# A linear-attention block with a sparse feed-forward: casts of weight sums moved ahead, row turns in pairs, and a later end for seven down products

## What is computed

```python
def attn(x, Wq, Wk, Wv, Wo):                 # 16 heads, 4 key/value heads, head size 128
    q, k, v = x @ Wq.T, x @ Wk.T, x @ Wv.T   # split into heads; RoPE on q and k
    qf, kf = elu(q) + 1, elu(k) + 1
    state, z = cumsum_s(kf[s] outer v[s]), cumsum_s(kf[s])
    out[s] = (qf[s] @ state[s]) / (qf[s] . z[s] + 1e-6)
    return out @ Wo.T

def ffn(x, w_gate, w_up, w_down):            # 512 -> 2048 -> 512
    h = silu(x @ w_gate) * (x @ w_up)
    h = keep_the_2_largest_of_every_4(h)     # by absolute value, along the 2048
    return h @ w_down

x = x + layernorm(attn(layernorm(x)))
x = x + layernorm(ffn(layernorm(x)))
```

## Time and profile before

| | |
|---|---|
| median of 3 runs | 1211.42 us (1211.18 to 1211.43) |
| the profiled execution | 1212.48 us |
| its span in the profile | 1210.5 us |
| mean granted TensorE clock | 0.989 of full speed |
| TensorE busy | 1172.4 us, 97% of the span |
| VectorE, ScalarE, GpSimd busy | 863.9, 521.0, 472.9 us (71%, 43%, 39%) |

### The profile page before, as it was taken

The page is one execution under the profiler, slowest core; times in us unless marked ns, Lnnn a source line. Parts: engine busy times, 40 slices in busy tenths (PEclk is TensorE's granted clock), DMA queues, the critical chain, the costliest instruction groups (busy, mean ns, idle before and its releaser), DMA issues.

```text
span 1210.5 us, 16282 instructions
## 1 busy us (share of the span) xinstructions
PE 1172.4 (97%) x5862; PEld 985.0 (81%) x5862; DVE 863.9 (71%) x1428; ACT 521.0 (43%) x1017; POOL 472.9 (39%) x381
## 2 busy tenths in 40 slices
PE   9999999999999999999999989798999999999986
PEld 7888888888888888888888778686888787888865
DVE  8944666756665457676576777888687778868798
ACT  5534544544545345444455333434423444333322
POOL 6421533525645125153355334453434533212224
PEclk9999999999999999999999989999999999999998
DMA  6321423313344133232246867665523564343421
GB/s 222 87 68 51 105 66 79 100 37 102 120 121 124 48 88 88 69 88 75 54 138 189 281 209 237 219 214 182 157 87 113 197 207 162 122 156 122 156 70 70
DMA packets 96367, 153.77 MB, mean 127 GB/s; under 512 B 10272, under 2 KB 31008, under 8 KB 96288
## 3 DMA queue, kind: packets, MB, share of 16 engines
q1 hardware_dynamic: 96288, 152.74, 40.9%
HBM read 96.60 MB, written 40.89 MB: 114 GB/s over the span
## 4 chain that ended last, share of the span: by engine, by line
PE 74%; DVE 15%; ACT 4%; issue 3%; DMA 1%; SPq 1%; POOL 1%; DVEq 0%; ACTq 0%
PE bank_q L812 8%; PE bank_q L814 8%; PE bank_q L813 8%; PE bank_y L814 5%; PE bank_y L813 5%; PE bank_y L812 5%; PE bank_od L1040 5%; PE bank_od L1043 4%; PE bank_t L812 3%; PE bank_t L814 3%; PE bank_t L813 3%; PE bank_s L937 2%; PE bank_s L812 2%; PE bank_s L813 2%; PE bank_s L814 2%
## 5 line engine op out<-in xcount | busy, mean ns | idle before, releaser
L812 PE MATMUL bank_q<-x_hi,w_hi 128*128 128x512 f32 x464 | 187.0, 403 | 1.0 <-ACT scratch L1343 0.9
L814 PE MATMUL bank_q<-x_lo,w_hi 128*128 128x512 f32 x464 | 182.0, 392 | 0.0
L813 PE MATMUL bank_q<-x_hi,w_lo 128*128 128x512 f32 x464 | 181.7, 392 | 0.0
L1944 POOL TENSOR_TENSOR w_lo<-stage,w_hi 128x512 fp32r<-128x512 f32 x60 | 78.8, 1323 | 123.8 <-ACT w_hi L1216 123.1
L1944 POOL TENSOR_TENSOR big_lo<-q_rows,big_hi 128x1024 fp32r<-128x1024 f32 x31 | 73.9, 2385 | 116.8 <-ACT big_hi L1255 116.8
L1944 POOL TENSOR_TENSOR big_lo<-hidden,big_hi 128x512 fp32r<-128x512 f32 x24 | 46.4, 1954 | 147.8 <-ACT big_hi L1389 100.2
L814 PEld LDWEIGHTS bank_q<-x_lo,w_hi 128*128 128x128 f32 x464 | 87.7, 189 | 19.1
L812 PEld LDWEIGHTS bank_q<-x_hi,w_hi 128*128 128x128 f32 x464 | 87.8, 189 | 18.3 <-ACT scratch L1343 1.8
L813 PEld LDWEIGHTS bank_q<-x_hi,w_lo 128*128 128x128 f32 x464 | 87.9, 189 | 16.8
L814 PE MATMUL bank_y<-wout_lo,a_hi 128*128 128x512 f32 x256 | 100.0, 391 | 0.0
L812 PE MATMUL bank_y<-wout_hi,a_hi 128*128 128x512 f32 x256 | 99.8, 390 | 0.0
(11 more groups left out here) (423 smaller groups left out, 3063.7 us busy)
## 6 DMA issues: line engine op xcount, KB each, us to landing
q_rows<-scratch SPq DMA_DIRECT2D x116, 128.0 KB, 2.4
x_rows<-x SPq DMA_DIRECT2D x40, 256.0 KB, 2.9
stage<-wq SPq DMA_DIRECT2D x32, 256.0 KB, 2.8
stage<-wo SPq DMA_DIRECT2D x32, 256.0 KB, 2.7
s_keep<-x_hi SPq DMA_DIRECT2D x16, 512.0 KB, 4.3
s_keep<-x_lo SPq DMA_DIRECT2D x16, 512.0 KB, 5.2
w_hi<-s_keep SPq DMA_DIRECT2D x32, 256.0 KB, 3.6
w_lo<-s_keep SPq DMA_DIRECT2D x32, 256.0 KB, 4.1
```

The lines of the kernel that those rows point to most:

```text
L812: pe.matmul(ps, whi, xhi, start=first, stop=False, skip_group_check=True)
L813: pe.matmul(ps, wlo, xhi, start=False, stop=False, skip_group_check=True)
L814: return pe.matmul(ps, whi, xlo, start=False, stop=last, skip_group_check=True)
L1944: return pool.tensor_tensor(dst, full, hi.bitcast(F32), ALU.subtract)
```

## The change

It has three parts.

1. ScalarE's cast of the sums of round r moves from the end of its slot S[r] + 1 to near its head, behind the casts of weights for down products and ahead of the absolute value. In `SUM_AT`, rounds 10 to 15 go from slots 13, 14, 15, 17, 18, 19 to 12, 13, 14, 15, 17, 18; by the formula above their loads, casts, low parts and stores move with them.
2. The eight row turns of the second batch go from slots 19, 20, 20, 21, 22, 23, 23, 24 into pairs in slots 19, 21, 23, 25; statistics and normalising move accordingly, and so do five of the first six steps of `combine_x` (from slots 25 to 27 into 26 and 27).
3. Down product 49 goes from slot 62 to slot 64, where six others already stand. VectorE adds it up at the head of slot 64 instead of in slot 63; in slot 64 three sums instead of one stand between the masks and the kept rows; the last kept rows and their low parts move from slot 66 to slot 65 on VectorE, as do the matching casts on ScalarE and the piece of this work on GpSimd.

```diff
--- before.py
+++ after.py
@@ -57,7 +57,7 @@
     if y >= LAST:
         return y + 9
     if y > 47:
-        return (60, 62)[y - 48] if y < 50 else SLOTS
+        return 60 if y == 48 else SLOTS
     return 8 * (y // 8) + 11 + min(y % 8, 6)
 
 
@@ -95,7 +95,7 @@
 
 
 
-SUM_AT = [0, 1, 2, 3, 5, 6, 7, 9, 10, 11, 13, 14, 15, 17, 18, 19]
+SUM_AT = [0, 1, 2, 3, 5, 6, 7, 9, 10, 11, 12, 13, 14, 15, 17, 18]
 
 
 def sum_place(r):
@@ -145,9 +145,9 @@
 ROWS = [j for j in JOBS[TT:-TT] if j[:2] != ("mid", 1)]
 IN_1 = [7, 10, 11, 14, 15, 18, 19, 22]
 MID_0 = [39, 42, 43, 46, 47, 50, 51, 54]
-MID_1 = [19, 20, 20, 21, 22, 23, 23, 24]
-STAT_1 = [16, 17, 17, 18, 20, 21, 21, 22]
-NORM_1 = [17, 18, 18, 19, 21, 22, 22, 23]
+MID_1 = [19, 19, 21, 21, 23, 23, 25, 25]
+STAT_1 = [17, 17, 18, 18, 21, 21, 23, 23]
+NORM_1 = [18, 18, 19, 19, 22, 22, 24, 24]
 
 
 def sum_tick(kind, b, t):
@@ -1367,6 +1367,9 @@
                 for k in pieces_at(tick, "d"):
                     if not last_down(PLAN[k][0]):
                         split(k)
+                for r in range(ROUNDS):
+                    if SUM_AT[r] + 1 == n:
+                        split_sums(r)
                 if 1 <= n <= EDGE:
                     i = (n - 1) % 4
                     g.wait_ge(dve_h, n)
@@ -1390,9 +1393,6 @@
                 for k in pieces_at(tick, "gud"):
                     if PLAN[k][0][0] != "d" or last_down(PLAN[k][0]):
                         split(k)
-                for r in range(ROUNDS):
-                    if SUM_AT[r] + 1 == n:
-                        split_sums(r)
                 if n in (28, 29):
                     cast_t(n - 28)
                 if EDGE <= n < SLOTS:
@@ -1427,7 +1427,6 @@
                     split_hidden(STEPS - 2)
                 if n == SLOTS + 1:
                     absolute(NU - 1, 1, 1)
-                if n == SLOTS + 2:
                     split_hidden(STEPS - 1)
                 for u in DOWN_AT:
                     for i in range(4):
@@ -1855,15 +1854,15 @@
                     pair_1(NU - 1, 1, 0)
                     add_down(downs[0])
                     keep_masks(NU - 1, 0)
-                    add_down(downs[1])
+                    for y in downs[1:4]:
+                        add_down(y)
                     keep_rows(NU - 1, 0)
                     hidden_lows(NU - 1, 0)
-                    for y in downs[2:]:
+                    for y in downs[4:]:
                         add_down(y)
                 if n == SLOTS + 1:
                     pair_1(NU - 1, 1, 1)
                     keep_masks(NU - 1, 1)
-                if n == SLOTS + 2:
                     keep_rows(NU - 1, 1)
                     hidden_lows(NU - 1, 1)
                 if n > SLOTS:
@@ -1877,7 +1876,7 @@
                 for r in range(ROUNDS):
                     if SUM_AT[r] == n:
                         sum_weights(r)
-                for step in {25: (0, 1), 26: (2, 3, 4), 27: (5,), 29: (6,), 30: (7,)}.get(n, ()):
+                for step in {26: (0, 1, 2), 27: (3, 4, 5), 29: (6,), 30: (7,)}.get(n, ()):
                     combine_x(step)
                 for job in at(tick, lambda j: add_tick(j) - 1, ENDING[-1:]):
                     q, sums_of = JOBS.index(job), Y[:, job[2], :]
@@ -2035,7 +2034,7 @@
                         hidden_lows(2 * (NU + v - 1) + late)
                 if n == SLOTS:
                     hidden_lows(STEPS - 2)
-                if n == SLOTS + 2:
+                if n == SLOTS + 1:
                     hidden_lows(STEPS - 1)
                 for u in DOWN_AT:
                     for i in range(4):
```

## The result

The changed kernel took 1205.3 us (median of 5, 1202.5 to 1207.6) against 1211.42: ratio 0.9946 (0.9929 to 0.9964). In two later comparisons, each beside the kernel before on one chip, it was 0.9935 (0.9922 to 0.9949) and 0.9936 (0.9923 to 0.9949), 7.6 and 7.9 us. So it is faster by 6 to 8 us, about half of the 15.7 forecast. The first median lies 1.3 us above the range, the two later ones (1203.7 and 1204.1) at its upper end. The profiled execution is the shortest of those five, 1202.5 us with a span of 1200.6.

The account below looks back on a forecast made before the run. The prediction held that only TensorE's waits, the lower clock behind them and VectorE's work at the end could move the time. Its terms, 6.9 + 2.3 - 0.6 + 7.1 + 0 = 15.7 us, gave 1195.7 us; range 1189 to 1204.

Parts of the forecast that it names:

- Term A: Up to TensorE's up product of slot 6: earlier casts bring L1790 of slot 5 forward and restore the clock, 6.9 us.
- the credit: Slot 2: moving the sums' adds off GpSimd's work saves half of 3.3 us, 1.7 us.
- this way to fail: Moved sums merely meet another GpSimd split, as VectorE and GpSimd exclude each other; the total would be 2.4 us smaller.
- The lower bound, 3.4: Worst case for the gain up to TensorE's up product of slot 6, the clock staying as it is: 3.4 us.
- Term B: TensorE's two other waits for L1790, after slot 6, go: 2.3 us, bounds 0.5 and 2.3.
- load and L1790 move with them, some 9.5 us: Round 8's load, behind VectorE's masks of slot 8, and L1790 of slot 13 come some 9.5 us earlier.
- Term C: TensorE's wait for GpSimd's low part of the down weight grows, lower clock as before: -0.6 us, bounds -1.3 and 6.4.
- Slots 15 to 18: Round 13's load lands at 783; L1790 of slot 17 starts at about 797.3, 2.4 us before TensorE needs it.
- The rival on loads: Round 13 or 12 lands 5 us later; TensorE waits 2 or 4 us at slots 17 and 18: 1198 to 1202; chance 0.24.
- Term D: Row turns in pairs: both waits of 1.1 and 4.5 us go, with 1.5 of clock: 7.1 us, bounds 5.6 and 7.1.
- Both waits go: TensorE's waits of 1.1 and 4.5 us at the row turns vanish, pairs' low parts being made a slot earlier.
- Edit 3: Seven down products last: 3.0 us TensorE hole in slot 62, VectorE's end unchanged: 0 us, bounds +1.1 and -1.8.

Follow-up runs that it names:

- the run with small low parts: Changed kernel with GpSimd making the low parts of rows 0 and 1 of the first batch's gated rows for 32 of 512 columns only: 1196.5 us, 0.9877.
- the run with the down weight ahead: Changed kernel with the last piece of the down weight split ahead of the gate and up pieces in slots 14 and 22: 1204.6 us, 0.9939.
- The run with that piece ahead: Kernel before with the turns in pairs and, in slot 22 alone, the down weight's last piece split ahead of gate and up pieces: 1203.7 us, 0.9939.
- the longer execution shown above: Profiled execution of the changed kernel run again with no edit: 1205.3 us, the longest of a run with median 1203.7.

## Why the prediction was wrong

**The reading of the bound was right**: TensorE's time moved only with its waits and the clock behind them, and the waits named were the ones that changed. Of the signs to look for, most came: 1.9 of 25.0 us for the cast and 15.8 for loads in their place, no wait at the turns, one of 5.2 us for the down weight, the hole at the end. The wait in slot 6 near 1 us without a lower clock behind it did not, and a second wait for a down weight was not forecast. Neither of the two signs of being wrong came: TensorE does not wait in slots 16 to 19, and the end does not change the time. What failed is the size of A, B and D.

**Term A, 6.9 forecast, 3.0 in the trace.** L1790 of slot 5 came at 696.10 instead of 699.15. By slots (starts of L1790 in both traces): slots 1 and 2 gave 3.9 us, against 1.4 + 1.7 forecast; slot 3 lost 1.5 where 0.8 was to be gained; slot 4 gave 0.6 instead of 1.2. The step that failed is the credit, "moving off GpSimd's work can add to it": the moved adds left GpSimd's splits, but VectorE's comparisons moved into them. Without the 1.7 of credit the forecast for L1790 is 3.4, near the 3.05 of this trace and the 3.3 of the run with small low parts, in which the splits met adds and not comparisons. The prediction had named this way to fail, with 2.4 us less in its sum, but had not taken it. The sum also had no term for GpSimd's low part of row 0, which had run in the idle time that was taken away: with it on VectorE, VectorE's product of slot 5 came at 695.18, 0.9 us earlier. With 3.1 us of wait left and not 1.0, the clock's 1.8 did not come back either. The lower bound, 3.4, was not low enough.

**Term B, 2.3 forecast, 0.4 in the trace** (TensorE came to its up product of slot 14 3.4 us earlier, to that of slot 6 3.0). VectorE started slot 13 at 765.40, 3.4 us earlier than before and not 9.5. Of the step "load and L1790 move with them, some 9.5 us" the link held and the size failed: VectorE's masks of slot 8 ended 3.6 us earlier (725.98 for 729.56) and the load of round 8 was there 3.8 us earlier (744.02 for 747.83). In VectorE's timeline:

```profile
744.02 0.43 DVE L1671 TENSOR_TENSOR x_part<-x_part 128x256 f32<-128x256 f32 x1 [4.99 <-DMA x_part<-wg]
...
765.40 0.68 DVE L1789 TENSOR_TENSOR hidden<-bank_q,scratch 128x512 f32<-128x512 f32 x1
```

The masks should have moved by the 5.1 of term A and 4.1 of cast waits. The first was 3.0, and what the casts gave in slots 6 and 7 went mostly to three adds that now met GpSimd's splits there, 1.4 to 1.5 us each for 0.42. Behind the masks VectorE waited 5.0 us for the load instead of 3.5.

**Term C, -0.6 forecast, -0.5.** The wait for the down weight went from 4.75 to 5.2 us, with the lower clock. That it comes out is partly luck: GpSimd's split started 1.9 us earlier and not 7.9 (777.79 for 779.71), and TensorE came 3.4 earlier and not 9.2, two errors of some 6 us that cancel.

**Slots 15 to 18.** L1790 of slot 17, forecast at about 797.3, came at 805.05. The load of round 13 was issued at 784.24, not 777. The wait for the load of round 12, 4.7 us, was not in the sum at all. This did not show in the time, as TensorE asked for that product only at 806.19, but it is what stopped the next gain, as the run with the down weight ahead shows. The rival on loads had the late loads, but TensorE's wait in slots 17 and 18 that it named did not come in the change itself. Its four rounds in a row with one slot of lead are three by the formula (11, 12 and 13).

**Term D, 7.1 forecast, 1.75 alone.** Both waits and their clock went, and 3.9 us with 2.5 of clock came for the next down weight, 1.2 to 1.7 us in the whole change. The step "Both waits go" was right and the sum stopped there: it did not ask what TensorE, earlier by that much, would meet next. The trace of the kernel before had the answer: 3.5 us to spare at the next down weight, for a gain of 7.1. The run with that piece ahead measured 7.5.

**Edit 3, 0 forecast, 0.1.** Hole of 2.9 us for 3.0; from VectorE's sum before it to its last add of a down product 50.8 us against 50.7.

In sum, 3.0 + 0.4 - 0.5 + 5.5 + 0 = 8.4 of the trace's terms (D with its 1.6 us of new wait) against 15.7: 3.9 are missing in A, 1.9 in B and 1.6 in D. The two profiled spans differ by 9.9 us; there the kernel before also lost 1.7 us to the lower clock at 1006 us (4.93 us busy at 0.66), where the change lost none. The medians give 6.1 to 7.9: the profiled execution is the shortest of its five, and the longer execution shown above lost more to the clock.

## What to carry to other kernels

An engine's idle time can be another's working time: before closing a wait on VectorE, look at what GpSimd does in it and who waits for that. Where a chain of waits is taken away one at a time, the price of each is only the distance to the next thing that is late, so walk the earlier engine forward through the trace, queue by queue, until nothing of the gain meets a later arrival (here 3.5 us were to spare for a gain of 7.1). When two late things hide each other, as the down weight and the loads here, undoing one shows nothing; both have to go in one version.

## What was not expected of the hardware

GpSimd's low part of 128 x 512 took 2.87 us in the kernel before and 4.00 in the change for the same work, ending 1.1 us after VectorE's last instruction in both. After nearly equal waits of TensorE (3.1 and 3.3 us) the lower clock cost 1.7 us in one execution and 2.9 in another of the same kernel. After waits of 3.1 us and more it fell in all of these traces. After waits of 2.2 to 2.9 us it fell in some (2.4 us with row 0 on VectorE: 0.53 in the 2.5 us behind it) and not in others (2.7 us with the small low parts: 1.00).
